# A transformer block of seven products per 2x2 blocking: product 1's operand C12 + C22 is added up in DRAM instead of on VectorE

## The chip, the cores and the metric

One core of one Trainium2 chip runs the kernel. The metric is the device time of one execution in microseconds (us). The times before are three runs: 1259.12 us median, 1258.83 the lowest, 1260.07 the highest.

## The reference

x is 32 x 64 x 1024 (batch, channel, time), float32. Two computations follow each other and the input is added to the result:

```python
W = weights[condition]                               # one 64x64 matrix per batch entry
y = jnp.einsum('bct,bcd->bdt', x, W)
h = jax.nn.gelu(jnp.einsum('bsd,df->bsf', y, inter_w) + inter_b, approximate=True)   # 1024 -> 4096
out = x + jnp.einsum('bsf,fd->bsd', h, output_w) + output_b                          # 4096 -> 1024
```

## The kernel before

The 2048 tokens are taken in two passes (h = 0 and 1) of 1024. Each of the two large products is blocked 2x2 and made with seven block products instead of eight (Strassen's scheme in Winograd's form), which needs sums of the input blocks. Each operand is split into a high and a low float32r part, so that one product is three matmuls.

**Stage 1** of a pass (`first`, L531) makes h = gelu(y W1 + b1). It runs over 8 groups g of 512 columns of W1, and in a group over 14 steps c (7 products, two halves p each), of 12 matmuls of 128x128 by 128x512. For each step ACT makes the high part of lhs (`high1`, L655) and DVE the low part (`low1`, L827), three buffers in turn. POOL makes the sums of W1's blocks that the products need (L479 to L496), for the following group: its waits are for DVE's lhs of that group's predecessor. The results are four tiles of a group, C11, C12, C22 and C21, each 128 x 2 x 512 float32 (512 KB) with one buffer. ACT copies partial results from PSUM into them (`copy1`, L668), DVE adds others (`add1`, L833) and ACT applies gelu in place. C12's gelu comes at steps 10 and 11 of the group, C22's at 12 and 13, and C11's and C21's trail into steps 0 to 2 of the next.

**Stage 2** (`second`, L571) is h W2, 7 products of 16 steps. Its left operands are seven tiles a group, kept in DRAM as `h_mem[h, product, g]`: C11, HS1, HS2, HS4, HS3, C21 and C22 for products 0 to 6, with HS1 = C12 + C22, HS3 = C11 - C12, HS2 = HS1 - C11 and HS4 = C21 - HS2. DVE makes the HS tiles (`combine`, L843) in the `trail` of a group, that is in steps 0 to 4 of the next group.

The order of the work is written out by hand: each engine has one queue, and semaphores tie them. What stands around the change:

- SyncE (SP) issues nearly all DMAs, in one order: at the start of group g C22's store of g-1 has just gone, then the two loads of W1 for g+1 (`load_w1`), then `keep_rest` for g-1, which stores HS1, C11, HS3, C21, HS2 and HS4, each behind its own wait. In pass 0 SP also moves the y operand of pass 1 through DRAM (y_mem, y_in). At a stage's end it loads h back, W2 and x.
- ACT copies new partial results into C11 at steps 4 and 5, into C22 at 6 and 7 and into C12 at 8 and 9 (`within`, L700). Before C22's first copy it waits for C22's store (L716). C12 has no wait of its own.
- PE's product 3 (step 6) waits for C22's copy (`p5_copied`, L550), product 2 (step 4) for C11's (L548), product 4 (step 8) for C12's (L552).
- The tiles of x that the second stage adds to lie where C11 to C21 were. SP loads the second four of them behind waits for these tiles' stores (L380 to L386).

Of the kernel before, what the change touches and what calls it, by code (L numbers as in the profile page):

```python
# [8 lines left out]
ALU = mybir.AluOpType  # L9
# [23 lines left out]
def build(nc, x, itok, cond_w, w1, b1, w2, b2, out):  # L33
# [32 lines left out]
    with ExitStack() as ctx:  # L66
# [3 lines left out]
        def sem(name):  # L70
            return ctx.enter_context(nc.semaphore(name))
# [53 lines left out]
        y1_kept = [sem(f"y1_kept{i}") for i in range(2)]  # L125
        y_in = [sem(f"y_in{i}") for i in range(PRODUCTS)]
        c11_kept, c21_kept, c22_kept = sem("c11_kept"), sem("c21_kept"), sem("c22_kept")
        hs_kept = [sem(f"hs_kept{i + 1}") for i in range(4)]
        out_kept = [sem(f"out_kept{i}") for i in range(5)]
        out_done, out_ended = sem("out_done"), sem("out_ended")  # L130
# [114 lines left out]
        def _(sp):  # L245
# [16 lines left out]
            def keep_rest(h, g):  # L262

                n = h * NG + g + 1
                sp.wait_ge(hs_made[0], n)
                keep(h, 1, g, hs1, hs_kept[0])
                sp.wait_ge(c11_gelu, 2 * n)
                keep(h, 0, g, c11, c11_kept)
                if g == NG - 1:
                    load_h(h, HRING)  # L270
                if (h, g) == (0, 0):
                    for i in range(2):
                        sp.wait_ge(y1_staged[i], 32 * TB)
                    sp.dma_start(y1_in[:], y_raw_mem[0]).then_inc(y1_back, 16)
                sp.wait_ge(hs_made[2], n)
                keep(h, 4, g, hs3, hs_kept[2])
                sp.wait_ge(c21_gelu, 2 * n)
                keep(h, 5, g, c21, c21_kept)
                if g == NG - 1:
                    load_h(h, HRING + 1)  # L280
                sp.wait_ge(hs_made[1], n)
                keep(h, 2, g, hs2, hs_kept[1])
                sp.wait_ge(hs_made[3], n)
                keep(h, 3, g, hs4, hs_kept[3])
# [61 lines left out]
            for h in range(PASSES):  # L346
                for g in range(NG):
                    if g + 1 < NG and (h, g) != (0, 0):
                        if (h, g) == (1, 0):
                            sp.wait_ge(out_kept[0], 16)  # L350
                            sp.wait_ge(out_kept[1], 16)
                        load_w1(h, g + 1)
                    if g > 0:
                        keep_rest(h, g - 1)
                    if (h, g) == (0, 2):
                        sp.dma_start(b2_all[:], b2.partition_broadcast(P)).then_inc(b2_in, 16)
                    if h == 0:
                        for c in range(CHUNKS):
                            if y1_item(g, c) is not None:
                                keep_y1(y1_item(g, c))  # L360
                    if g == NG - 1:
                        for n in range(HRING):
                            load_h(h, n)
                        sp.wait_ge(step_done, step1(h, g, 4))
                        for half in range(2):
                            load_w2("11", half)
                        sp.wait_ge(step_done, step1(h, g, 8))
                        for half in range(2):
                            load_w2("12", half)
                    sp.wait_ge(c22_gelu, 2 * (h * NG + g + 1))  # L370
                    keep(h, 6, g, c22, c22_kept)
                keep_rest(h, NG - 1)

                for n in range(HRING + 2, PRODUCTS * NG):
                    load_h(h, n)
                    if n == 6:
                        sp.wait_ge(lhs_lo, step1(h, NG - 1, CHUNKS))
                        for j in range(TB):
                            load_x(h, j)
                    if n == 7:  # L380
                        sp.wait_ge(c11_kept, 16 * (h + 1) * NG)
                        sp.wait_ge(c21_kept, 16 * (h + 1) * NG)
                        sp.wait_ge(c22_kept, 16 * (h + 1) * NG)
                        sp.wait_ge(hs_made[3], (h + 1) * NG)
                        for j in range(TB, TILES):
                            load_x(h, j)  # L386
                    if n == 8:
                        sp.wait_ge(step_done, step1(h, NG - 1, 12))
                        for half in range(2):
                            load_w2("22", half)  # L390
                    if n == 12:
                        sp.wait_ge(step_done, step1(h, NG - 1, CHUNKS))
                        for half in range(2):
                            load_w2("21", half)
                    if h == 0:
                        if n == 44:
                            sp.wait_ge(t_made[2], PAIRS)
                            sp.wait_ge(rhs_lo, rhs_n(h, 4))
                            load_y(4)
                            load_y(5)  # L400
                        if n == 46:
                            sp.wait_ge(rhs_lo, rhs_n(h, 5))
                            load_y(2)
                            load_y(3)
                        if n == 52:
                            sp.wait_ge(t_made[3], PAIRS)
                            load_y(0)
                            load_y(1)
                    if n == 45:
                        sp.wait_ge(b2_added, (h + 1) * TILES)  # L410
                        sp.wait_ge(acc_added, (h * PRODUCTS + 4) * 2)
                        store(h, 3, out_kept[0] if h == 0 else out_done)
                    if n == 47:
                        sp.wait_ge(acc_added, (h * PRODUCTS + 5) * 2)
                        store(h, 4, out_kept[2] if h == 0 else out_done)
                    if n == 54:
                        sp.wait_ge(acc_added, (h * PRODUCTS + 6) * 2)
                        store(h, 5, out_kept[1] if h == 0 else out_done)
                if h == 0:
                    sp.wait_ge(rhs_lo, rhs_n(h, 6, PAIRS // 2))  # L420
                    load_w1(1, 0)
                    m, n = QUARTER[6]
                    cols = slice(n * BANK, (n + 1) * BANK)
                    for u in range(2):
                        sp.wait_ge(acc_added, PRODUCTS * 2 - 1 + u)
                        rows = slice(4 * m + 2 * u, 4 * m + 2 * u + 2)
                        sp.dma_start(out_tok[0, :, rows, cols], acc[:, rows, cols]).then_inc(out_kept[3 + u], 16)
                    load_y(6)
# [13 lines left out]
        def _(pool):  # L442
# [10 lines left out]
            def picks1(first_j, end_j):  # L453
# [2 lines left out]
                    nc.gpsimd.tensor_copy(to, of).then_inc(picked1, 1)  # L456
                pool.wait_ge(picked1, end_j * PER)

            picks1(0, TILES)
            for h in range(PASSES):  # L460
                for g in range(NG):
# [32 lines left out]
                    pool.wait_ge(s_made[1], n + 1)  # L494
                    nc.gpsimd.tensor_tensor(s4_w[:], a12, s2_w[:], ALU.subtract).then_inc(s_made[3], 1)  # L495
                    nc.gpsimd.tensor_tensor(a21, a11, a21, ALU.subtract).then_inc(s_made[2], 1)  # L496


        @block.tensor
# [128 lines left out]
        def _(act):  # L628
# [71 lines left out]
            def within(h, g, c):  # L700
# [12 lines left out]
                if c in (6, 7):  # L713
                    p = c - 6
                    if g > 0 and p == 0:
                        act.wait_ge(c22_kept, 16 * n)  # L716
                    if (h, g, p) == (1, 0, 0):
                        act.wait_ge(out_kept[4], 16)
                    copy1(h, g, 2 + p, p, c22, p5_copied)
                if c in (8, 9):  # L720
                    copy1(h, g, c - 4, c - 8, c12, s2_copied)
                if c in (10, 11):
                    p = c - 10
# [83 lines left out]
        def _(dve):  # L807
# [38 lines left out]
            def trail(h, g, c):  # L846
                n = h * NG + g + 1
                if c == 0:
                    add_c11(h, g, 1)
                    dve.wait_ge(c12_gelu, 2 * n)  # L850
                    dve.wait_ge(c22_gelu, 2 * n)
                    if n > 1:
                        dve.wait_ge(hs_kept[0], 16 * (n - 1))
                    combine(hs1, c12, c22, ALU.add, hs_made[0])
                if c == 2:
                    dve.wait_ge(c11_gelu, 2 * n)
                    if n > 1:
                        dve.wait_ge(hs_kept[2], 16 * (n - 1))
                    combine(hs3, c11, c12, ALU.subtract, hs_made[2])
                if c == 3:  # L860
                    dve.wait_ge(hs_made[0], n)
                    if n > 1:
                        dve.wait_ge(hs_kept[1], 16 * (n - 1))
                    combine(hs2, hs1, c11, ALU.subtract, hs_made[1])
                if c == 4:
                    dve.wait_ge(c21_gelu, 2 * n)
                    dve.wait_ge(hs_made[1], n)
# [166 lines left out]
```

## Time and profile before

| | us |
|---|---|
| span of the profiled execution | 1257.8 |
| time of the profiled execution | listed only as its span |
| three runs, lowest / median / highest | 1258.83 / 1259.12 / 1260.07 |
| PE busy | 1252.9 |
| DVE busy | 834.8 |
| ACT busy | 567.4 |
| POOL busy | 185.8 |
| moved by DMA | 249.28 MB, mean 198 GB/s |
| DMAs issued from POOL | none |

The chain of work that ended last is PE for 99% of the span. The engines other than PE matter only where PE would have to wait for them; a queue, though, also waits in its own order, so each wait is read with what stands behind it.

### The profile page before, as it was taken

How to read it: one execution, taken by the hardware profiler on the slowest of the kernel's cores; microseconds unless marked ns; L12 is line 12 of the kernel's file. 1: busy time of each engine (PE TensorE's matmuls, PEld its weight loads, DVE VectorE, ACT ScalarE, POOL GpSimd, SP SyncE). 2: the span in 40 equal slices, each digit the busy share in tenths (PEclk: the TensorE clock that was granted, in tenths of full speed). 3: DMA queues.
4: the chain of work that ended last, by engine and by line, in shares of the span. 5: the costliest groups of instructions: out<-in, count | busy, mean ns of one | idle time of the engine just before them, and what ended most of it. 6: DMA issues, size and time to landing. Idle time of an engine off the chain costs nothing.

```text
span 1257.8 us, 15365 instructions
## 1 busy us (share of the span) xinstructions
PE 1252.9 (100%) x5660; PEld 1042.7 (83%) x5660; DVE 834.8 (66%) x1092; ACT 567.4 (45%) x969; POOL 185.8 (15%) x92
## 2 busy tenths in 40 slices
PE   9999999999999999999999999999999999999999
PEld 8888888888888888888888888888888888888887
DVE  6977777676577777656657455554547767784764
ACT  4745554454544444444434434444444444444442
POOL 3362223321000000000034233322200000000000
PEclk9999999999999999999999999999999999999999
DMA  9576655764997222249834324554189932222431
GB/s 340 172 266 247 244 196 221 280 251 181 382 391 283 100 87 99 101 165 362 309 141 178 111 117 174 184 184 143 74 326 406 347 131 97 101 101 95 157 128 57
DMA packets 94876, 249.28 MB, mean 198 GB/s; under 512 B 7346, under 2 KB 16850, under 8 KB 93394
## 3 DMA queue, kind: packets, MB, share of 16 engines
q1 hardware_dynamic: 94080, 248.01, 54.2%
q8 instruction: 46, 0.75, 0.2%
q10 hardware_dynamic: 722, 0.28, 0.1%
q14 instruction: 28, 0.23, 0.1%
HBM read 162.28 MB, written 85.98 MB: 197 GB/s over the span
## 4 chain that ended last, share of the span: by engine, by line
PE 99%; DMA 1%; SPq 0%; DVE 0%; issue 0%
PE ps L566 48%; PE ps L582 48%; PE ps L526 1%; PE ps L511 1%; DMA x<-in_x_dram 1%; PE ps L601 0%; SPq L328 0%; SPq L329 0%; SPq L326 0%; DVE acc L1011 0%
## 5 line engine op out<-in xcount | busy, mean ns | idle before, releaser
L566 PE MATMUL ps<-y,lhs 128*128 128x512 f32 x2688 | 611.0, 389 | 0.0
L582 PE MATMUL ps<-rhs,lhs 128*128 128x512 f32 x2664 | 604.2, 389 | 0.0
L566 PEld LDWEIGHTS ps<-y,lhs 128*128 128x128 f32 x2688 | 504.1, 188 | 104.7 <-issue 0.2
L582 PEld LDWEIGHTS ps<-rhs,lhs 128*128 128x128 f32 x2664 | 500.0, 188 | 103.8
L738 ACT ACTIVATE lhs<-h_raw 128x512 fp32r<-128x512 f32 x224 | 141.6, 632 | 345.9 <-PE ps L582 340.3
L889 DVE TENSOR_TENSOR lhs<-h_raw,lhs 128x512 fp32r<-128x512 f32 x224 | 155.1, 693 | 188.5 <-ACT lhs L738 188.5
L830 DVE TENSOR_TENSOR lhs<-w_raw,lhs 128x512 fp32r<-128x512 f32 x128 | 117.7, 921 | 124.6 <-ACT lhs L666 124.5
L666 ACT ACTIVATE lhs<-w_raw 128x512 fp32r<-128x512 f32 x128 | 80.9, 633 | 167.3 <-PE ps L566 161.9
L892 DVE TENSOR_TENSOR rhs<-W,rhs 128x512 fp32r<-128x512 f32 x224 | 153.2, 684 | 0.0
L830 DVE TENSOR_TENSOR lhs<-s_w,lhs 128x512 fp32r<-128x512 f32 x96 | 91.4, 955 | 88.2 <-ACT lhs L666 88.1
L479 POOL TENSOR_TENSOR s_w<-w_raw 128x1024 f32<-128x1024 f32 x16 | 48.6, 3038 | 623.4 <-PE ps L582 354.0
L747 ACT ACTIVATE rhs<-W 128x512 fp32r<-128x512 f32 x224 | 137.9, 616 | 0.0
L666 ACT ACTIVATE lhs<-s_w 128x512 fp32r<-128x512 f32 x96 | 60.5, 631 | 123.1 <-PE ps L566 121.0
L921 DVE TENSOR_TENSOR W<-W,W 128x512 f32<-128x512 f32 x128 | 87.5, 684 | 0.0
L675 ACT ACTIVATE c<-c,b_col 128x512 f32<-128x512 f32 x96 | 68.2, 711 | 7.2 <-DVE c L837 7.2
L837 DVE TENSOR_TENSOR c<-ps,c 128x512 f32<-128x512 f32 x96 | 65.4, 681 | 0.0
L672 ACT ACTIVATE c<-ps 128x512 f32<-128x512 f32 x96 | 56.2, 585 | 5.6 <-DMA h_mem<-c 5.6
L495 POOL TENSOR_TENSOR s_w<-w_raw,s_w 128x1024 f32<-128x1024 f32 x16 | 41.7, 2605 | 38.4 <-DVE lhs L830 37.9
L496 POOL TENSOR_TENSOR w_raw<-w_raw 128x1024 f32<-128x1024 f32 x16 | 46.2, 2886 | 0.0
L487 POOL TENSOR_TENSOR s_w<-s_w,w_raw 128x1024 f32<-128x1024 f32 x16 | 40.8, 2552 | 36.1 <-DVE lhs L830 35.6
L844 DVE TENSOR_TENSOR hs<-c,c 128x1024 f32<-128x1024 f32 x32 | 40.5, 1267 | 0.0
L908 DVE TENSOR_TENSOR acc<-ps,acc 128x1024 f32<-128x1024 f32 (+1 forms) x29 | 33.6, 1161 | 2.3 <-PE ps L601 2.3
(37 smaller groups left out, 301.7 us busy)
## 6 DMA issues: line engine op xcount, KB each, us to landing
h_raw<-h_mem SPq DMA_DIRECT2D x112, 512.0 KB, 3.3
h_mem<-hs SPq DMA_DIRECT2D x64, 512.0 KB, 4.4
W<-in_L_ffn_output_w_dram SPq DMA_DIRECT2D x32, 1024.0 KB, 12.8
w_raw<-in_L_ffn_inter_w_dram SPq DMA_DIRECT2D x31, 1024.0 KB, 8.6
h_mem<-c SPq DMA_DIRECT2D x48, 512.0 KB, 5.4
y_mem<-y_out SPq DMA_DIRECT2D x28, 512.0 KB, 3.1
y<-y_mem SPq DMA_DIRECT2D x7, 2048.0 KB, 12.9
acc<-in_x_dram SPq DMA_DIRECT2D x16, 512.0 KB, 8.4
```

The source lines that it names most:

```text
L566: last = nc.tensor.matmul(ps[:, bank, :], w[:, k, :], y[i][:, part, k, :], start=(i in FRESH and k == 0 and u == 0), stop=(k == KH - 1 and ...
L582: last = nc.tensor.matmul(ps[:, bank2(h, j, tb), :], lhs[s % RING][:, a, blk(tb)], rhs[r][:, w, :], start=(j in FRESH and q == 0 and u == ...
L666: nc.scalar.activation(split1(s, 0), w1_part(h, g, c), ACT.Copy).then_inc(lhs_hi, 1)
L672: nc.scalar.activation(to[:, p, :], ps[:, bank1(h, g, role, p), :], ACT.Copy).then_inc(copied, 1)
L675: nc.scalar.activation(tile[:, p, :], of, ACT.Gelu_apprx_tanh, bias=b1_col[:, 4 * g + 2 * m + p:4 * g + 2 * m + p + 1]).then_inc(made, 1)
L738: nc.scalar.activation(lhs[s % RING][:, 0, :], of, ACT.Copy).then_inc(lhs_hi, 1)
L747: nc.scalar.activation(rhs[r][:, 0, :], w2_part(j, q), ACT.Copy).then_inc(rhs_hi, 1)
L830: nc.vector.tensor_tensor(split1(s, 1), w1_part(h, g, c), split1(s, 0).bitcast(F32), ALU.subtract).then_inc(lhs_lo, 1)
L837: nc.vector.tensor_tensor(tile[:, p, :], ps[:, bank, :], tile[:, p, :], ALU.add).then_inc(added, 1)
L889: nc.vector.tensor_tensor(lhs[s % RING][:, 1, :], of, lhs[s % RING][:, 0, :].bitcast(F32), ALU.subtract).then_inc(lhs_lo, 1)
L892: nc.vector.tensor_tensor(rhs[r][:, 1, :], w2_part(j, q), rhs[r][:, 0, :].bitcast(F32), ALU.subtract).then_inc(rhs_lo, 1)
L921: nc.vector.tensor_tensor(to[:, pair], a[:, pair], b[:, pair], ALU.subtract).then_inc(t_made[n], 1)
```

## The change

The sum C12 + C22 is no longer made by DVE in HS1. SP stores C12 itself into `h_mem[h, 1, g]`, as soon as its gelu is done, and GpSimd issues a DMA that adds C22 to it there. The DMA is issued after POOL's sums of the next group, for the last group after those of its predecessor. HS2, which was HS1 - C11, becomes C22 - HS3, which is the same (C22 + C12 - C11). Waits are added on ACT, before C22 and C12 are written again, and on SP, before x is loaded over them.

```diff
         c11_kept, c21_kept, c22_kept = sem("c11_kept"), sem("c21_kept"), sem("c22_kept")
+        c12_kept = sem("c12_kept")
...
                 n = h * NG + g + 1
-                sp.wait_ge(hs_made[0], n)
-                keep(h, 1, g, hs1, hs_kept[0])
+                sp.wait_ge(c12_gelu, 2 * n)
+                keep(h, 1, g, c12, c12_kept)
...
                         sp.wait_ge(hs_made[3], (h + 1) * NG)
+                        sp.wait_ge(c12_kept, 16 * (h + 1) * NG)
+                        sp.wait_ge(hs_kept[0], 16 * (h + 1) * NG)
...
+            def add_c22(h, g):
+
+                n = h * NG + g + 1
+                pool.wait_ge(c22_gelu, 2 * n)
+                pool.wait_ge(c12_kept, 16 * n)
+                pool.dma_start(h_mem[h, 1, g], c22[:].rearrange("p b t -> p (b t)"), accum_op=ALU.add).then_inc(hs_kept[0], 16)
+
...
                     nc.gpsimd.tensor_tensor(a21, a11, a21, ALU.subtract).then_inc(s_made[2], 1)
+                    if g > 0:
+                        add_c22(h, g - 1)
+                add_c22(h, NG - 1)
...
                     if g > 0 and p == 0:
                         act.wait_ge(c22_kept, 16 * n)
+                        act.wait_ge(hs_kept[0], 16 * n)
+                        act.wait_ge(hs_made[1], n)
...
                 if c in (8, 9):
+                    if n > 0 and c == 8:
+                        act.wait_ge(c12_kept, 16 * n)
+                        act.wait_ge(hs_made[2], n)
                     copy1(h, g, c - 4, c - 8, c12, s2_copied)
...
                     add_c11(h, g, 1)
-                    dve.wait_ge(c12_gelu, 2 * n)
-                    dve.wait_ge(c22_gelu, 2 * n)
-                    if n > 1:
-                        dve.wait_ge(hs_kept[0], 16 * (n - 1))
-                    combine(hs1, c12, c22, ALU.add, hs_made[0])
                 if c == 2:
                     dve.wait_ge(c11_gelu, 2 * n)
+                    dve.wait_ge(c12_gelu, 2 * n)
...
                 if c == 3:
-                    dve.wait_ge(hs_made[0], n)
+                    dve.wait_ge(hs_made[2], n)
+                    dve.wait_ge(c22_gelu, 2 * n)
...
-                    combine(hs2, hs1, c11, ALU.subtract, hs_made[1])
+                    combine(hs2, c22, hs3, ALU.subtract, hs_made[1])
```

## Rows read from the trace of the kernel before

**Rows 1.** The page's busy times: us, share of the span, instructions.

```profile
PE 1252.9 (100%) x5660; PEld 1042.7 (83%) x5660; DVE 834.8 (66%) x1092; ACT 567.4 (45%) x969; POOL 185.8 (15%) x92
```

**Rows 2.** The chain of waits in order of time: start us, us, what.

```profile
63.63 277.45 PE ps L566 x1224
341.09 304.64 PE ps L582 x1344
645.73 304.64 PE ps L566 x1344
```

**Rows 3.** Timeline of ACT, pass 1, g=5: start us, us, instruction, [idle before it].

```profile
823.10 0.71 ACT L675 ACTIVATE c<-c,b_col 128x512 f32<-128x512 f32 x1
...
847.58 0.58 ACT L672 ACTIVATE c<-ps 128x512 f32<-128x512 f32 x1
...
852.48 0.63 ACT L666 ACTIVATE lhs<-w_raw 128x512 fp32r<-128x512 f32 x1 [1.60 <-PE ps L566]
```

**Rows 4.** Timeline of DVE, pass 1, g=5: the first three combinations, a late lhs.

```profile
832.60 1.21 DVE L844 TENSOR_TENSOR hs<-c,c 128x1024 f32<-128x1024 f32 x1
...
837.44 1.22 DVE L844 TENSOR_TENSOR hs<-c,c 128x1024 f32<-128x1024 f32 x1
...
840.16 1.22 DVE L844 TENSOR_TENSOR hs<-hs,c 128x1024 f32<-128x1024 f32 x1
842.27 1.92 DVE L830 TENSOR_TENSOR lhs<-s_w,lhs 128x512 fp32r<-128x512 f32 x1 [0.89 <-ACT lhs L666]
```

**Rows 5.** Timeline of SP's DMA issues, pass 1, g=5.

```profile
829.64 1.39 SPq L256 DMA_DIRECT2D w_raw<-in_L_ffn_inter_w_dram  x2
833.84 0.34 SPq L260 DMA_DIRECT2D h_mem<-hs  x1
```

**Rows 6.** DMA issues of 829.5 to 831.2 and 833.5 to 834.5 us: KB, landing.

```profile
w_raw<-in_L_ffn_inter_w_dram SPq DMA_DIRECT2D x2, 1024.0 KB, 7.4
...
h_mem<-hs SPq DMA_DIRECT2D x1, 512.0 KB, 6.1
```

**Rows 7.** Timeline of POOL, pass 1, g=5: the first sum for g+1.

```profile
840.41 3.22 POOL L479 TENSOR_TENSOR s_w<-w_raw 128x1024 f32<-128x1024 f32 x1 [22.08 <-DVE lhs L830]
```

**Rows 8.** All stores of line L260: issue ns min/median/max, starts; their landing.

```profile
L260 SPq DMA_DIRECT2D h_mem<-c x48: 319/338/977, 67.7 to 953.9; - x48
...
DMA to landing us min/median/max: 2.6/4.9/10.9
```

**Rows 9.** The page's DMA issues: count, KB each, median us to landing.

```profile
h_mem<-hs SPq DMA_DIRECT2D x64, 512.0 KB, 4.4
...
w_raw<-in_L_ffn_inter_w_dram SPq DMA_DIRECT2D x31, 1024.0 KB, 8.6
...
y<-y_mem SPq DMA_DIRECT2D x7, 2048.0 KB, 12.9
```

**Rows 10.** Pass 0, g=4: SP's issue of HS1's store, and its landing.

```profile
186.48 0.34 SPq L260 DMA_DIRECT2D h_mem<-hs  x1
...
h_mem<-hs SPq DMA_DIRECT2D x1, 512.0 KB, 10.6
```

**Rows 11.** Timeline of POOL and ACT, pass 0, g=4.

```profile
195.95 3.04 POOL L479 TENSOR_TENSOR s_w<-w_raw 128x1024 f32<-128x1024 f32 x1 [23.73 <-DMA w_raw<-in_L_ffn_inter_w_dram]
...
198.31 0.60 ACT L672 ACTIVATE c<-ps 128x512 f32<-128x512 f32 x1 [3.43 <-DMA h_mem<-c]
```

**Rows 12.** The end of pass 1's stage 1: SP's issues, and the first one's landing.

```profile
943.52 0.34 SPq L260 DMA_DIRECT2D h_mem<-c  x1
...
965.93 1.75 SPq L316 DMA_DIRECT2D acc<-in_x_dram  x4
...
h_mem<-c SPq DMA_DIRECT2D x1, 512.0 KB, 10.4
```

**Rows 13.** Timeline of ACT, pass 0, g=2.

```profile
128.57 0.63 ACT L757 ACTIVATE y_out<-y_in 128x512 fp32r<-128x512 f32 x1 [3.93 <-DMA y_mem<-y_out]
```

## The prediction

> **What bounds the kernel now.** I read the busy shares first: PE is busy for 1252.9 of 1257.8 us, DVE, the next, for 834.8 [rows 1]. Then the chain of waits in order of time, to see whether PE only looks busy: from 63.63 us on it is PE alone, 277.45 us for 1224 matmuls, 304.64 for 1344, and 304.64 for 1344 again [rows 2]. Each piece is 226.7 ns a matmul, in both stages alike: PE waits for nothing after the prologue. So no engine that is relieved can bring time. The change can only leave PE alone or stall it, and what remains is to find each new wait and measure its slack.
>
> The unit is a step of 12 matmuls, 12 x 226.7 ns = 2.72 us, and a group g of 14 steps, 38.08 us. I work in one quiet group, pass 1, g=5, whose step 0 starts on PE at 645.73 + 5 x 38.08 = 836.13 us; step 6 starts 16.32 us later, at 852.45. ACT's row agrees: its lhs for step 8 is released by PE, when step 5 has ended, at 852.48 [rows 3].
>
> **The change part by part.**
> *DVE* loses the C12 + C22 combination, 1.21 us in each of 16 groups, 19.4 us in all [rows 4]. Its other two keep their number and length. HS2 becomes C22 - HS3, made right after HS3: HS3 ends at 837.44 + 1.22 = 838.66 and HS2 starts at 840.16 today [rows 4], so the new order costs no wait. PE does not wait for DVE. Worth: 0.
>
> *SP's store of product 1* moves. It waited for HS1 (DVE 832.60 + 1.21, issued 833.84) and now waits for C12's gelu, whose last half ends at 823.10 + 0.71 = 823.81, long before SP is there [rows 3 to 5]. SP issues it right behind the two w1 loads, at 829.64 + 1.39 = 831.03. Of the rest of SP's queue nothing waits longer: C11's store is still held by C11's gelu. C12 lands behind w1 (second load: about 830.65 + 7.4 = 838.0), and no later than HS1, which was issued after it and landed at 833.84 + 6.1 = 839.9 [rows 5, 6]. I take 839.0.
>
> *POOL* then issues the accumulating DMA. In its queue this stands behind the sums of group g and ahead of the first sum for g+1. Today POOL waits 22.08 us for DVE before that sum starts at 840.41 [rows 7], so waiting for C12 until 839.0 costs nothing. The issue itself is in no row of POOL; the nearest, SP's, take 0.32 to 0.98 us [rows 8]. Even several us more would meet a sum that is first used by g+1, whose step 0 starts at 874.21. Worth: 0.
>
> *The accumulate*: call T the time from C12's landing to the accumulate's landing, the issue included. It reads 512 KB of C22, reads 512 KB of h_mem and writes 512 KB, and no such operation is in the trace. Low end: a plain 512 KB store at its fastest, 2.6 us [rows 8]. High end: a 2048 KB load, 12.9 us, plus the longest issue, 0.98, makes 13.9 [rows 8, 9]. The median 512 KB store takes 4.4 and a 1024 KB load 8.6 [rows 9]. Three movements of 512 KB of which two can overlap lie between these, nearer to the second; I take 7.
>
> The Trainium skill (DMA: Bandwidth & Descriptors, section "Anatomy of one DMA — SWDGE (gpsimd) path") fits such a DMA from GpSimd with 2.0 us plus its bytes over 436e3: an estimate of 3.2 us for 512 KB, near the 2.6 of the row. It counts no read of the destination. By it nothing at all would stall and the sum would be without the half microsecond below.
>
> *Who waits for it*: ACT, before it copies the next first half of C22, today at 847.58 and without idle [rows 3]. Behind ACT's wait stand the second half and lhs of steps 7 and 8. PE needs the first half at step 6, 852.45; the copy takes 0.58, so ACT has to be let go by 851.87. The lhs of step 7 would then be done by ACT at 853.1 and by DVE at 853.8 (0.69 each), up to 855.0 if POOL's sums hold DVE to the 1.92 of the row [rows 4], and step 7 starts at 855.17. Slack: 851.87 - 839.0 = 12.9 us against T = 7; the accumulate lands at 846.0, before ACT even asks. This stands 14 times (g = 1 to 7 of two passes). Without that cover each microsecond of T over 12.9 costs 14 us. C12's own buffer, free from 846.0 at the latest, is written again only behind the lhs of 852.48: 0.
>
> *The tightest group* is pass 0, g=4. A load of y_in goes ahead of w1 there, w1 lands only at 195.95, where POOL's wait of 23.73 us ends, and ACT stands 3.43 us before its C11 copy, until C11's store lands at 198.31 [rows 11]. PE's step 0 is at 341.09 - 4 x 38.08 = 188.77, step 4 at 199.65, so that copy (0.60) had 0.7 us left. C12 will land between w1, 195.95, and where HS1 did, 186.48 + 10.6 = 197.1 [rows 10, 11]; say 196.5. For C22 the limit is step 6 less the copy, 205.09 - 0.60 = 204.5: slack 8.0 against T = 7, so 0. But from about 197 on the accumulate shares the DMA engines with C11's last 1.3 us. If each gets half, C11 lands 1.3 later, at 199.6, against a limit of 199.05: 0.5 us of stall. I count 0.5.
>
> *At a stage's end* the last C22 store is issued at 943.52 and takes 10.4 us, to 953.9; C12 follows by some 955, the accumulate by 962. SP's new waits stand ahead of the second four loads of x, which go at 965.93 [rows 12]: 0. At T = 13.9 they would go 3 us later, and are first used when product 0 of the stage is done, at 950.37 + 16 x 2.72 = 993.9.
>
> Sum: 0 + 0 + 0 + 0.5 + 0. The profiled execution has a span of 1257.8 us; no time of its own is given apart from that, and the three runs stand 1.0 to 2.3 us over it, the median 1.3. So 1257.8 + 0.5 + 1.3 = 1259.6 us.
>
> **The rivals.**
> B, every group stalls: T is over 12.9 us, because reading, adding and writing follow one another. Place: ACT's wait before the C22 copy; it decides from T = 12.9. At 13.9 it costs 13 x 1.0 + (13.9 - 8.0) = 18.9 us, so 1278. At 16, beyond my bound, 13 x 3.1 + 8.0 = 48, so 1307. For it: the operation is in no row, and w1 and four stores fill the DMA engines just then. Against it: it would be slower than loads of 2048 KB. Chance 0.13.
>
> C, only the crowded groups of pass 0 stall: T of 9.5 gives 1.5 us at g=4, T of 12.9 gives 4.9. At g=2, ACT waited 3.93 us for a y_mem store, until 128.57 [rows 13]; behind it stand y_out and lhs on DVE, done at 128.57 + 0.63 + 0.69 + 0.69 = 130.6, and step 7 starts at 341.09 - 6 x 38.08 + 19.04 = 131.65: room for 1.1 us, of which the accumulate's traffic could eat 1 to 2. So 1260.6 to 1265. For it: rooms of 0.7, 1.1 and 8.0 us. Against it: each is one place. Chance 0.12, three quarters of it beyond 0.2%.
> A row near to it: a lhs of DVE takes 1.92 in place of 0.69 us when POOL's sum runs beside it [rows 4, 7]. The Trainium skill (SBUF — State Buffer, section "A bandwidth-pool intuition that's wrong (but worth ruling out)") has a DMA of GpSimd at about 3100 ns in place of 620 when a DVE copy keeps its descriptors from being written. As an estimate that adds 2.5 us to T, which gives C and not B. DVE runs two-operand instructions in this stage, so the rows bear it out little.
>
> D, faster: DVE's 19.4 us come through. It would take a gap on PE and rows 2 have none; only the first 63.63 us have any, and the change does not touch them. Chance 0.03, at most 3 us, 1256.
>
> A, the forecast: chance 0.72.
>
> **How the numbers follow.** 0.2% is 2.5 us, about what a measurement of this kernel can tell from no change. Faster 0.03 (D); same 0.72 + 0.03 of C = 0.75; slower 0.13 + 0.09 = 0.22. The range starts at 1258.0, under the fastest run shown, and goes to 1268: all of A and C and the mildest part of B (T = 13.2 costs 13 x 0.3 + 5.2 = 9.1, so 1268). Most of B and D, some 0.15, is left out.
>
> **What would show it.** Right: the stages again at 226.7 ns a matmul; ACT without idle before its C22 copies, but for pass 0; 48 combinations on DVE instead of 64; accumulates that land 5 to 9 us after C12; POOL's first sums still released by DVE's lhs or at most 2 us later. Wrong: ACT waiting over 4.3 us for a POOL DMA in a quiet group, with stage 1 of pass 1 longer than 304.64 us; or C12 landing much after 839 in that group.

## The result: 0.4 to 0.5% slower, lost in three groups of pass 0

The changed kernel takes 1265.4 us (median of 4 runs, 1264.43 to 1266.03) against 1258.97 (4 runs); the ratio of the runs is 1.0044, 95% interval [1.0032, 1.0057]; the two medians themselves stand 6.4 us or 0.51% apart. Measured again beside the experiments it was 1264.94 against 1259.09, ratio 1.0042 [1.0029, 1.0056], 0.46% between the medians. The 1265.4 us are inside the range (1258.0 to 1268.0) and 5.8 us over the predicted 1259.6: the likeliest case, no difference, had a chance of 0.72 and is not what happened. The measured time is rival C's, whose 1260.6 to 1265 ends about there. The range held because it was drawn to take in all of rival C, not because the likeliest case was right.

The profiled execution has a span of 1263.1 us (its own time 1264.89). The page after, busy times and the kind of DMA queue that was not there before:

```profile
PE 1255.0 (99%) x5660; PEld 1042.9 (83%) x5660; DVE 840.9 (67%) x1076; ACT 568.8 (45%) x969; POOL 192.6 (15%) x108
...
q0 software_dynamic: 2304, 8.39, 3.7%
...
h_mem<-c SPq DMA_DIRECT2D x64, 512.0 KB, 6.6
...
h_mem<-hs SPq DMA_DIRECT2D x48, 512.0 KB, 5.0
...
h_mem<-c POOLq DMA_DIRECT2D x16, 512.0 KB, 7.9
```

DVE has 16 instructions fewer, and yet it is busy for 6.1 us more than in [rows 1]. The 19.4 us that went are more than made up by the lhs instructions, which POOL holds up longer: the two groups of line L848 have a mean of 1013 and 1094 ns, against 921 and 955 before.

The chain of waits, in order of time (start us, us, what), against [rows 2]:

```profile
64.29 54.46 PE ps L579 x240
...
217.91 76.44 PE ps L579 x336
294.39 51.96 PE ps L579 x228
346.36 304.64 PE ps L595 x1344
651.00 304.64 PE ps L579 x1344
```

Stage 1 of pass 1 takes 304.64 us as before. Stage 1 of pass 0 ends at 346.36 instead of 341.09, 5.27 us later; 0.66 of that stood already at 64.29 (before: 63.63), in the prologue and group g=0, and 4.6 us are lost in the groups behind. Both kernels have the same 5382 matmuls of the two large products in the trace, so each can be paired with its fellow. What the distance grows by from a group's first matmul to the next group's is PE's loss in that group. The tables of PE's loss below are made so, in us, one profiled execution each. From g=1 of pass 0 on, groups and stages not shown lost 0.00 in every kernel.

| | g=1 | g=2 | g=3 | g=4 | g=5 | g=6 | pass 1 | sum |
|---|---|---|---|---|---|---|---|---|
| changed kernel | 0.03 | 1.76 | 0.03 | 2.47 | 0.00 | 0.32 | 0.00 | 4.61 |
| changed kernel, again | 0.05 | 2.51 | 0.00 | 2.49 | 0.00 | 0.51 | 0.00 | 5.55 |

The two rows are the same kernel. For the second I had expected 1.3 to 1.8 us in g=2; it lost 2.51, so a difference under 0.75 us in g=2 between two kernels says little. The prologue and g=0 together differ from before by up to 0.8 us either way, in the kernel whose pass 0 is unchanged by +0.7, so nothing is read from them.

**Pass 0, g=4.** Timelines of POOL, ACT and PE's weight loads (start us, us, instruction, [idle before <- releaser]), against [rows 11]:

```profile
200.43 0.90 POOL L467 DMA_DIRECT2D h_mem<-c  x1 [24.41 <-DMA h_mem<-c]
201.04 2.73 POOL L489 TENSOR_TENSOR s_w<-w_raw 128x1024 f32<-128x1024 f32 x1
...
201.06 0.60 ACT L685 ACTIVATE c<-ps 128x512 f32<-128x512 f32 x1 [3.71 <-DMA h_mem<-c]
...
208.51 0.60 ACT L685 ACTIVATE c<-ps 128x512 f32<-128x512 f32 x1 [5.32 <-issue]
...
209.16 1.01 PEld L579 LDWEIGHTS ps<-y,lhs 128*128 128x128 f32 x5 [2.02 <-ACT c L685]
```

C12's store, issued at 186.98, lands at 199.8. POOL issues at 200.43, the accumulate lands 8.0 us later, at 208.4, and ACT stands 5.32 us before its C22 copy. PE's weight loads wait 2.0 us for that copy, and PE loses 1.8 there.

**Pass 0, g=2.** Here the path has more links. Timelines of POOL, DVE, SP, ACT and PE's weight loads:

```profile
118.98 0.88 POOL L467 DMA_DIRECT2D h_mem<-c  x1 [20.95 <-DMA h_mem<-c]
119.59 2.71 POOL L489 TENSOR_TENSOR s_w<-w_raw 128x1024 f32<-128x1024 f32 x1
...
119.43 3.43 DVE L848 TENSOR_TENSOR lhs<-s_w,lhs 128x512 fp32r<-128x512 f32 x1 [0.89 <-ACT lhs L679]
122.78 1.21 DVE L862 TENSOR_TENSOR hs<-c,hs 128x1024 f32<-128x1024 f32 x1
...
124.38 0.43 SPq L357 DMA_DIRECT2D b_all<-in_L_ffn_output_b_dram  x1
124.86 8.35 SPq L312 DMA_DIRECT2D y_mem<-y_out  x3
...
127.13 0.60 ACT L685 ACTIVATE c<-ps 128x512 f32<-128x512 f32 x1 [2.29 <-DMA h_mem<-c]
131.32 0.63 ACT L775 ACTIVATE y_out<-y_in 128x512 fp32r<-128x512 f32 x1 [3.59 <-DMA y_mem<-y_out]
...
133.39 2.59 PEld L579 LDWEIGHTS ps<-y,lhs 128*128 128x128 f32 x12 [1.48 <-ACT c L685]
```

The same of the kernel before, DVE and SP:

```profile
118.75 1.92 DVE L830 TENSOR_TENSOR lhs<-s_w,lhs 128x512 fp32r<-128x512 f32 x1 [0.89 <-ACT lhs L666]
...
122.20 0.44 SPq L356 DMA_DIRECT2D b_all<-in_L_ffn_output_b_dram  x1
122.68 7.78 SPq L311 DMA_DIRECT2D y_mem<-y_out  x3
```

POOL's sum starts behind its DMA and holds DVE's lhs to 3.43 us (1.92 before): in every kernel this lhs ends 0.55 us after POOL's sum. HS4 and its store are late by that, and behind that store SP issues b2's load and then y_mem's store, at 124.86; before it was 122.68, 1.5 us earlier once the 0.69 is off by which the group itself starts later. It lands 6.4 us later, at 131.2, ACT makes y_out only then [rows 13: 128.57], and the second C22 copy and lhs behind it are late for PE. It is the place that rival C named, with 1.1 us of room; a table below shows that PE begins to lose at some 0.3.

### The profile page after: what moved, and what is told of

It is laid out like the page before. It is cut to its first block, busy times and chain, and to the rows that moved or that the text cites. A ratio compares the mean times of both kernels' runs of the same rounds, so it can differ in the third digit from the quotient of the medians.

```text
span 1263.1 us, 15398 instructions
## 1 busy us (share of the span) xinstructions
PE 1255.0 (99%) x5660; PEld 1042.9 (83%) x5660; DVE 840.9 (67%) x1076; ACT 568.8 (45%) x969; POOL 192.6 (15%) x108
## 4 chain that ended last, share of the span: by engine, by line
PE 94%; DMA 2%; DVE 2%; issue 2%; SPq 0%; ACT 0%; ACTq 0%; POOLq 0%
PE ps L595 48%; PE ps L579 43%; DMA h_mem<-c 1%; PE ps L524 1%; PE ps L539 1%; DMA y_mem<-y_out 1%; DVE lhs L848 1%; DVE y_out L950 1%; PE ps L614 0%; PE ps L622 0%; DVE hs L862 0%; ACT y_out L775 0%; DVE y_in L944 0%; DVE c L855 0%; SPq L257 0%
## 5 line engine op out<-in xcount | busy, mean ns | idle before, releaser
L848 DVE TENSOR_TENSOR lhs<-w_raw,lhs 128x512 fp32r<-128x512 f32 x128 | 129.3, 1013 | 120.7 <-ACT lhs L679 120.5
L848 DVE TENSOR_TENSOR lhs<-s_w,lhs 128x512 fp32r<-128x512 f32 x96 | 104.5, 1094 | 75.7 <-ACT lhs L679 75.5
L489 POOL TENSOR_TENSOR s_w<-w_raw 128x1024 f32<-128x1024 f32 x16 | 43.4, 2710 | 328.3 <-PE ps L595 293.4
L467 POOL DMA_DIRECT2D h_mem<-c x16 | 14.3, 893 | 357.1 <-DMA h_mem<-c 313.9
L950 DVE TENSOR_TENSOR y_out<-y_in,y_out 128x512 fp32r<-128x512 f32 x28 | 28.0, 1000 | 18.7 <-ACT y_out L775 18.2
```

Source lines behind the costliest of these rows:

```text
L848: nc.vector.tensor_tensor(split1(s, 1), w1_part(h, g, c), split1(s, 0).bitcast(F32), ALU.subtract).then_inc(lhs_lo, 1)
```

## The experiments

The question was which of four things takes the 4.6 us: SP's new store, POOL's waits and issue, the landing of the accumulate behind which ACT waits, or its traffic beside the y_mem store.

**Only SP's and DVE's part.** GpSimd does nothing new.

```diff
-                    if g > 0:
-                        add_c22(h, g - 1)
-                add_c22(h, NG - 1)
...
-                        act.wait_ge(hs_kept[0], 16 * n)
```

> Only SP's part and DVE's part of the change: C12 is stored in place of HS1, HS2 = C22 - HS3, ACT's added wait for C12's store stands; GpSimd does nothing new, so C22 is missing from product 1's operand. Theory (the time goes to ACT's wait for the accumulate in pass 0, g=4, and to POOL's sum being moved in g=2): none of it is left, 1259.0 us, stage 1 of pass 0 unstretched. Rival 1 (the earlier store of C12 already disturbs w1, C11 or the y traffic): 1260 to 1262, with PE stalled in g=2 or g=4. Rival 2 (a fixed price of having a DMA on GpSimd, in the prologue and after the last instruction, 1.1 us): also 1259.0 here, prologue 0.66 us shorter than in the changed kernel.

Measured: 1259.1 us against 1259.54, ratio 0.9997 [0.9988, 1.0006]; no group loses anything. Storing C12 earlier and the new HS2 are free, as forecast.

**POOL waits, without a DMA.** The waits of ACT and SP for the accumulate go too.

```diff
-                pool.dma_start(h_mem[h, 1, g], c22[:]..., accum_op=ALU.add).then_inc(hs_kept[0], 16)
```

> As the changed kernel, but GpSimd only waits for C22's gelu and C12's landing and issues no DMA (C22 is missing from product 1's operand; ACT waits for no accumulate). Theory: POOL's first sum is still late behind C12's landing, so DVE's lhs in g=2 is still held to about 3.4 us and PE loses about 1.8 us there; nothing at g=4: 1260.8 us. Rival (the accumulate's own traffic delays the y_mem store in g=2): no stall there, 1259.0.

Measured: 1258.92 us, ratio 0.9998 [0.9989, 1.0007], every loss 0.00. The expectation of the theory, 1.8 us in g=2, did not come: POOL's sum starts 0.4 us later against PE's work than before, but takes 0.4 less, and DVE's lhs is unchanged. C12 landed 4.7 us after the group's first matmul here and 5.3 in the changed kernel, so the wait was also a shorter one. The timelines of POOL and DVE in g=2:

```profile
116.59 2.84 POOL L487 TENSOR_TENSOR s_w<-w_raw 128x1024 f32<-128x1024 f32 x1 [22.09 <-DMA h_mem<-c]
...
118.06 1.92 DVE L845 TENSOR_TENSOR lhs<-s_w,lhs 128x512 fp32r<-128x512 f32 x1 [0.89 <-ACT lhs L677]
```

**A tiny DMA of GpSimd** behind the same waits, to a spare tensor.

```diff
-                pool.dma_start(h_mem[h, 1, g], c22[:]..., accum_op=ALU.add).then_inc(hs_kept[0], 16)
+                pool.dma_start(spare[h, g], c22[:, 0, 0:16]).then_inc(hs_kept[0], 16)
```

> The changed kernel with GpSimd's accumulating DMA replaced by a tiny one of 64 bytes a partition of C22 to a spare tensor, behind the same waits and waited for by ACT in the same way (C22 is missing from product 1's operand). It keeps POOL's issue and takes the traffic and the long landing away. Theory as it now stands (two causes: POOL's issue pushes its first sum by about 1.2 us onto DVE's lhs, which holds HS4, SP and the y_mem store in g=2; and the accumulate's traffic and landing): lhs in g=2 still 2.9 to 3.4 us instead of 1.92, SP's y_mem store 1.0 to 1.4 us later, PE loses 0.2 to 0.6 us there and nothing at g=4: 1259.4 to 1259.9 us. Rival (issue costs nothing, traffic is all of it): lhs 1.92 us, no stall, 1259.0.

Measured: 1259.19 us against 1259.09, ratio 1.0001 [0.9992, 1.001]; 0.05 us in g=2, nothing elsewhere. The issue takes 0.56 us of POOL and DVE's lhs 2.16 us instead of 1.92, where 2.9 to 3.4 were expected; C12 landed early here, 4.4 us after the group's first matmul. So waits and a short issue cost next to nothing in these two runs. The issue of the accumulating DMA takes 0.88 us, and neither run had C12 as late as in the changed kernel; whether the 512 KB DMAs make it late is not shown: with the change in pass 0 alone it landed after 4.6 us.

**A plain DMA of GpSimd** of the full size.

```diff
-...accum_op=ALU.add).then_inc(hs_kept[0], 16)
+...).then_inc(hs_kept[0], 16)
```

> The changed kernel with a plain DMA of GpSimd in place of the accumulating one (it overwrites C12 in DRAM, so C12 is missing from the sum). Waits and issues are the same. If reading the destination is what makes the accumulate take 7 to 9 us, it lands in 4 to 5.5 us and pass 0, g=4 loses 0 to 0.5 us instead of 2.4; g=2's 1.8 us and the fixed part stay: 1263 us. If the queue of GpSimd or the crowd on the DMA engines sets it, it lands as before in 7 to 8 us and the time is 1265.

Measured: 1260.36 us against 1259.54, ratio 1.0006 [0.9997, 1.0015]. It lands in 5.7 us (median) where the accumulating one takes 7.9, and its issue takes 0.57 us where that takes 0.88:

```profile
h_mem<-c POOLq DMA_DIRECT2D x16, 512.0 KB, 5.7
```

g=2 loses 0.57 and g=4 1.03 us, 1.6 in all. The direction is that of the expectation, but I had put 1263 us, with g=2 unchanged and at most 0.5 lost in g=4. In g=2 y_mem's store takes no longer than before; it is issued 0.9 us later, behind a lhs of 2.87 us. Against the changed kernel's 4.6 and 5.6 us, 3 to 4 us come from the DMA's being an accumulating one, its longer issue included.

**Two buffers for C22.** Odd groups use HS1's old place, so ACT waits only for the accumulate of two groups ago.

```diff
-                        act.wait_ge(hs_kept[0], 16 * n)
+                        act.wait_ge(sum_two[g % 2], 16 * (n // 2))
...
-                    copy1(h, g, 2 + p, p, c22, p5_copied)
+                    copy1(h, g, 2 + p, p, c22s[g % 2], p5_copied)
```

> The changed kernel with two buffers for C22 (the second in HS1's old place, used by odd groups), so ACT waits for the accumulate of the group before the last, long landed; all sums are complete. Theory: pass 0, g=4's loss of 2.4 us and all ACT waits before C22's copies go, g=2's 1.8 us stays since POOL's order is untouched: 1263 us. Rival (contention of the accumulate with w1 and C11's store): PE still stalls at g=4, behind C11's copy, 1265.

Measured: 1261.18 us against 1259.54, ratio 1.0014 [1.0005, 1.0023]. g=4 loses 0.00, g=2 2.45, g=6 0.25. ACT waits as long as ever for C11's store in g=4 (3.73 us) but not for C22, and PE not at all: the loss of g=4 is the single buffer's, and not contention at C11's copy. The expectation of 1263 was 2 us too high; it counted from 1265.4, of which about 1 us is found in no group.

**Two buffers, and POOL's issue behind its first sum.**

```diff
                     nc.gpsimd.tensor_tensor(s1_w[:], a21, a22, ALU.add).then_inc(s_made[0], 1)
+                    if g > 1:
+                        add_c22(h, g - 2)
...
-                    if g > 0:
-                        add_c22(h, g - 1)
+                add_c22(h, NG - 2)
                 add_c22(h, NG - 1)
```

> Two buffers for C22 and the accumulate issued behind POOL's first sum for the next group instead of ahead of it; all sums complete. POOL's first sum starts at its old time, so DVE's lhs in g=2 is 1.92 us again and SP issues y_mem's store in time. Theory: what is left of g=2's 2.3 us (two buffers alone) is what the accumulate's traffic does to the y_mem store's landing, 0 to 1.3 us: 1259.2 to 1260.5. Rival (traffic is all of it): 1261.2 as with the two buffers alone.

Measured: 1261.27 us against 1259.09, ratio 1.0017 [1.0008, 1.0026]. DVE's lhs is back at 1.92 us, and g=2 loses 1.01 in place of 2.45; but g=3 loses 0.37 and g=6 1.00, and the sum is about the same. The change in pass 0 alone, with the issue in its first place, lost 0.54 and 1.03 there too. Timelines of DVE, SP and ACT in g=2:

```profile
119.24 1.92 DVE L857 TENSOR_TENSOR lhs<-s_w,lhs 128x512 fp32r<-128x512 f32 x1 [0.89 <-ACT lhs L688]
...
123.21 9.07 SPq L318 DMA_DIRECT2D y_mem<-y_out  x3
...
130.38 0.63 ACT L784 ACTIVATE y_out<-y_in 128x512 fp32r<-128x512 f32 x1 [5.25 <-DMA y_mem<-y_out]
```

SP issues the store in time, and it still takes 7.1 us to land where it took 5.8 before. So g=2's loss has two parts, and all kernels together give their sizes. The first y_mem store of g=2 against the kernel before, measured from the group's first matmul, in us:

| | issued later | takes longer | lands later | PE's loss in g=2 |
|---|---|---|---|---|
| changed kernel | 1.5 | 0.6 | 2.1 | 1.76 |
| changed kernel, again | 1.5 | 1.3 | 2.8 | 2.51 |
| pass 0 alone | 0.8 | 1.3 | 2.1 | 1.85 |
| two buffers | 1.4 | 1.3 | 2.8 | 2.45 |
| two buffers, issue behind the sum | 0.0 | 1.3 | 1.3 | 1.01 |
| one buffer, issue behind the sum | 0.3 | 1.2 | 1.6 | 1.23 |
| plain DMA | 0.9 | 0.0 | 0.9 | 0.57 |
| tiny DMA | 0.2 | 0.1 | 0.3 | 0.05 |

PE's loss is the delay of this landing less 0.3 us in every row. The first column is the way through POOL, DVE and SP's order. The second stands only where a DMA accumulates beside the store; that shared traffic makes it is the likely reading, and no run separates it from other ways.

The same store explains g=6, with 1.4 us of room in place of 0.3: in the changed kernel's two traces it landed 1.7 and 1.9 us later there (losses 0.32 and 0.51), in pass 0 alone and with two buffers and the issue behind the sum 2.4 (1.03 and 1.00).

**The change in one pass alone.** The other pass keeps HS1 on DVE.

```diff
+                    if h != 1:
+                        ...
+                        combine(hs1, c12, c22, ALU.add, hs_made[0])
...
+                    if g > 0 and h == 1:
+                        add_c22(h, g - 1)
```

> The change in pass 1 alone, pass 0 as before. Theory: ACT's waits for the accumulate in pass 1 stay under their slack of 4.3 us in all seven groups (3.0 at most in the changed kernel), so PE loses nothing: the time of before, within 0.5 us. Rival (a DMA on GpSimd has a price of its own somewhere outside the groups): 0.7 to 1.8 us more.

Measured, in pass 1 alone: 1259.19 us against 1259.09, ratio 1.0002 [0.9993, 1.0011]; all losses 0.00, with 8 accumulates in the run. In a pass with room, the accumulating DMA has no price.

> The change in pass 0 alone, pass 1 as before; the complement of the kernel with it in pass 1 alone, which showed no loss. Theory: all of the loss is here: 5 us of stall in pass 0's first stage at g=2, g=4 and g=6, about 1264.9 us. Rival (the two passes' parts add up to less than the whole): 1262.

Measured, in pass 0 alone: 1264.63 us against 1258.93, ratio 1.0043 [1.0028, 1.0059], the whole of it.

**One buffer, issue behind the first sum.** The same move of the issue as with two buffers, and nothing else:

```diff
+                    if g > 1:
+                        add_c22(h, g - 2)
```

> The changed kernel with one buffer for C22, but the accumulate issued behind POOL's first sum for the next group, 3.0 to 3.6 us later in quiet groups. It tests the slack I priced (ACT let go by 851.87 us in the quiet group, or a stall a group): before, POOL's sum ends at 843.6; issue at 843.6, landing 6.9 to 8 us later, at 850.5 to 851.6, so ACT waits 3 to 4 us in each of pass 1's seven groups and PE loses 0 to 0.5 us a group there, 0 to 3 in all; in pass 0 g=4 loses about 5 us in place of 2.4 and other groups 0 to 1 each. Time 1267 to 1271. If the limit is wrong and later by a step: 1265 as before.

Measured: 1265.45 us against 1258.93, ratio 1.0059 [1.0044, 1.0074], below the 1267 to 1271 expected: ACT waits 1.2 to 2.9 us before its C22 copies in pass 1 where I expected 3 to 4, and g=4 loses 2.62 where I expected 5. Pass 1 loses nothing. In pass 1's g=2, POOL and ACT show why, this kernel first, the changed one below:

```profile
734.14 0.89 POOL L467 DMA_DIRECT2D h_mem<-c  x1
...
739.41 0.60 ACT L686 ACTIVATE c<-ps 128x512 f32<-128x512 f32 x1 [1.17 <-DMA h_mem<-c]
```

```profile
732.70 0.88 POOL L467 DMA_DIRECT2D h_mem<-c  x1 [22.92 <-DMA h_mem<-c]
...
739.88 0.60 ACT L685 ACTIVATE c<-ps 128x512 f32<-128x512 f32 x1 [1.17 <-DMA h_mem<-c]
```

Issued 1.4 us later by these clocks, 1.9 us later against PE's work, it lands at the same moment. Over the six groups g=1 to g=6 of pass 1 it was issued 0.8 to 3.0 us later and landed between 0.6 us earlier and 1.3 later. So the time from issue to landing is no fixed term, and I had added it to a later issue as if it were. That it waits behind other stores would explain it, but is not shown.

**b2's load moved** out of g=2, on top of the two buffers.

```diff
-                    if (h, g) == (0, 2):
+                    if (h, g) == (0, 5):
                         sp.dma_start(b2_all[:], b2.partition_broadcast(P)).then_inc(b2_in, 16)
```

> Two buffers for C22, and SP's load of b2 (512 KB, just ahead of y_mem's store in pass 0, g=2) moved to g=5; all sums complete. Theory (g=2's remaining loss of 2.3 us comes through SP's order and the crowd around the y_mem store): that store is issued 0.5 us earlier and lands 1 us sooner, g=2 loses 0.5 to 1 us, the whole 1259.8 to 1260.3 us. Rival (the loss is set by DVE's lhs of 3.4 us and POOL, wherever the store goes): 1261.2.

Measured: 1262.01 us against 1258.93, ratio 1.0024 [1.0014, 1.0033], no better than two buffers alone. But the trace shows why: g=2 loses 0.00, with DVE's lhs still at 3.23 us, and g=5 loses 1.94. SP and ACT in g=5:

```profile
237.52 0.43 SPq L363 DMA_DIRECT2D b_all<-in_L_ffn_output_b_dram  x1
238.00 8.86 SPq L318 DMA_DIRECT2D y_mem<-y_out  x3
...
244.96 0.63 ACT L783 ACTIVATE y_out<-y_in 128x512 fp32r<-128x512 f32 x1 [6.18 <-DMA y_mem<-y_out]
```

Neither of the two expectations came (0.5 to 1 us in g=2; 1261.2 wherever the store goes): the loss went with the load. In both groups tried, the one with b2 between HS4's store and y_mem's pays. So it went, for the last run, where no y_mem store follows:

```diff
-                    if (h, g) == (0, 2):
+                    if (h, g) == (0, 7):
```

> Two buffers for C22, and b2's load in pass 0's last group, g=7, which has no y_mem store behind it (with b2 in g=5 the loss of 1.9 us was gone from g=2 and stood in g=5). All sums complete. Theory: the loss with two buffers is b2's load between HS4's store and y_mem's store, pushed over its 1.1 us of room by the accumulate; now neither g=2 nor g=5 loses anything and only g=6's 0.2 to 0.4 us is left: 1259.2 to 1259.6 us, no difference from before. Rival (any crowded group loses, whatever SP loads there): 1260.5 to 1261.

Measured: 1259.98 us against 1259.03, ratio 1.0006 [0.9996, 1.0015]: not to be told from before, though 0.4 us over the range expected. No group loses more than 0.05 us; the expected 0.2 to 0.4 us in g=6 is gone as well.

| PE's loss, us | g=1 | g=2 | g=3 | g=4 | g=5 | g=6 | sum |
|---|---|---|---|---|---|---|---|
| waits only | 0.00 | 0.00 | 0.00 | 0.00 | 0.00 | 0.00 | 0.00 |
| tiny DMA | 0.00 | 0.05 | 0.00 | 0.00 | 0.00 | 0.00 | 0.05 |
| plain DMA | 0.00 | 0.57 | 0.00 | 1.03 | 0.00 | 0.00 | 1.61 |
| pass 0 alone | 0.00 | 1.85 | 0.54 | 2.90 | 0.00 | 1.03 | 6.31 |
| one buffer, issue behind the sum | 1.01 | 1.23 | 0.07 | 2.62 | 0.44 | 0.13 | 5.51 |
| two buffers | 0.00 | 2.45 | 0.03 | 0.00 | 0.00 | 0.25 | 2.73 |
| two buffers, issue behind the sum | 0.00 | 1.01 | 0.37 | 0.00 | 0.00 | 1.00 | 2.39 |
| two buffers, b2 in g=5 | 0.00 | 0.00 | 0.05 | 0.02 | 1.94 | 0.13 | 2.14 |
| two buffers, b2 in g=7 | 0.00 | 0.00 | 0.00 | 0.00 | 0.00 | 0.05 | 0.05 |

No version beats the kernel before, and none could by this way: behind the prologue PE has no gap that DVE's 19.4 us could fill.

## Why the prediction was right and wrong

- **PE bounds it, nothing can be gained.** Right. Even without any loss the kernels stand at the time of before.
- **DVE's and SP's parts are worth 0.** Right, shown by the run with them alone.
- **POOL's issue is worth 0.** Near it for a short issue behind an early C12 (tiny DMA, 0.05 us). Wrong in the changed kernel: I asked only who needs POOL's sum, and not whom the sum holds up while it runs. It started 2.0 us later in g=2 and 2.6 in g=4, held by C12's landing, where I had given it 2 at most. Shifted, it kept DVE's lhs for 3.43 us instead of 1.92, and HS4, SP's queue and ACT were behind it. I had the row of 1.92 us and used it only for lhs of step 7.
- **T = 7 us, slack 12.9 us, 14 times.** The size was right for the quiet groups, if low: T is 7.5 to 8.5 us in g=1 to g=6 of pass 1. C12 came in g=5 at 840.1, where I took 839.0 (845.4 less the 5.27 of shift), and the accumulate landed at 847.7 in place of 846.0, when ACT asks and not before. In four other groups of pass 1 ACT waits for it, 7.6 us together and 3.0 at most; I had said that it would stand idle in pass 0 only. The limit of 4.3 us held, and rival B, at 0.13, did not come.
- **g=4, slack 8.0, 0.5 us of stall.** The step that failed in size: the term was 0 at C22's copy. C12 landed at 199.8, which is 197.3 on the clock of before (196.5 predicted), and T was 8.6 us (7). The two overruns, 0.8 + 1.6, against 1.0 of slack left make 1.4 us; PE's wait at step 6 came to 1.8, and with the steps behind it g=4 lost 2.47. The half microsecond that I did count, at C11's copy, did not occur: with two buffers ACT waits 3.73 us there and PE none.
- **g=2.** The step that failed in kind. I had the place right, as rival C, and in the likeliest case gave it no term at all. Its room was 0.8 us before step 7, not 1.1, and the three steps behind lose up to 0.5 more. Rival C gave the traffic beside the store 1 to 2 us (0.6 to 1.3 measured) and had no term for the way through POOL, DVE and SP's order. Measured 1.76 and 2.51 us in two executions, with b2's load between HS4's store and y_mem's.
- **The chances.** Two places with 0.7 and 1.1 us of room, and a slack of 8.0 us of which my own T took 7.0, stood against a cost known only between 2.6 and 13.9. On those rows 0.12 for C against 0.72 for A was too confident.
- **The two rules.** The accumulates landed 5.1 us after the issue at the least and 7.9 in the median, the plain DMAs 2.9 and 5.7. The 3.2 us estimated from the Trainium skill (DMA: Bandwidth & Descriptors, section "Anatomy of one DMA — SWDGE (gpsimd) path") agree with the fastest plain one within 10% and are less than half of an accumulating one in this crowd. GpSimd's issue took 0.87 to 1.02 us in all 16 places. The starved descriptors of which the Trainium skill tells (SBUF — State Buffer, section "A bandwidth-pool intuition that's wrong (but worth ruling out)") are not to be seen in that time; DVE ran no copies in this stage, so no run here tests them.

The last microsecond is open: the changed kernel is 5.9 to 6.4 us slower in the medians and 4.6 to 5.6 us are found on PE. The profiled executions scatter by 1.5 us in the prologue and g=0, which may be all of it.

## What to carry to other kernels

Where one engine is never idle, price a change by its narrowest rooms and not by the typical group: list each wait that has under 2 us left once the change is in, and follow everything that the change delays or crowds into it, down each engine's queue. A large transfer that no engine waits for can still cost, through the store that stands beside it. A buffer whose reader becomes a chain of two DMAs (store, then accumulate) is held for both: a second copy of it took g=4's 2.5 us away here.

## What was not expected of the hardware

- An accumulating DMA of 512 KB from SBUF to DRAM landed 7.9 us after its issue (median of 16, 5.1 to 9.4), a plain one at the same place in 5.7 (2.9 to 8.8). The issue takes 0.88 us of GpSimd against 0.57.
- Its time from issue to landing is not fixed: issued 1.9 us later in one group, it ended at the same time, and a y_mem store beside it took 1.2 to 1.3 us longer in five traces of six.
- GpSimd stood still for some 0.6 us between C12's landing and the start of its DMA (199.8 to 200.43).
- A sum of GpSimd in its way made 0.69 us of a two-operand instruction of DVE into 3.43. In g=2 of pass 0 the instruction ended 0.55 us after the sum in all kernels.
